# Moving the PSUM strip of a sequential recurrence's matmul from partitions 0 to 31 to partitions 96 to 127

## What is computed

```python
Wx = jnp.einsum('bti,hi->bth', x, W)
Wx = ((flat - mean) * jax.lax.rsqrt(var + BN_EPS) * gamma + beta).reshape(B, T, H)
Vt = V.T

def step(yt, wx_t):
    yt = jax.nn.sigmoid(wx_t + yt @ Vt)
    return (yt, yt)
...
_, ys = jax.lax.scan(step, y0, jnp.swapaxes(Wx, 0, 1))
```

## Time and profile before

| | |
|---|---|
| median of 3 runs | 986.31 us (983.46 to 988.56) |
| the profiled execution | 980.51 us |
| its span, first to last instruction | 978.7 us |
| mean granted TensorE clock over the span | 0.975 |
| PE / ACT / DVE / POOL busy | 900.6 / 447.5 / 414.0 / 239.3 us |
| the L2 recurrence, first matmul to last sigmoid | 411.9 to 901.3 us |

### The profile page before, as it was taken

The page is one execution under the profiler, slowest core; times in us unless marked ns, Lnnn a source line. Parts: engine busy times, 40 slices in busy tenths (PEclk is TensorE's granted clock), DMA queues, the critical chain, the costliest instruction groups (busy, mean ns, idle before and its releaser), DMA issues. The chain is left out here.

```text
span 978.7 us, 15448 instructions
## 1 busy us (share of the span) xinstructions
PE 900.6 (92%) x6248; PEld 514.2 (53%) x6248; DVE 414.0 (42%) x711; ACT 447.5 (46%) x1492; POOL 239.3 (24%) x144
## 2 busy tenths in 40 slices
PE   7958888889989987899999999999999999999976
PEld 4426766667754443344444444455555544554543
DVE  4599999999966645500000000002005400202753
ACT  4687777777735442233333333333333333334642
POOL 3239999999820000200000000000000000000410
PEclk9989999999999997899999999999999999999987
DMA  3020000000000000200000000000000000000000
GB/s 81 11 55 1 1 1 1 1 1 1 1 6 2 1 24 11 82 1 1 2 1 1 1 1 1 1 1 1 1 1 1 1 1 1 1 1 2 1 25 11
DMA packets 10320, 8.30 MB, mean 8 GB/s; under 512 B 7346, under 2 KB 8610, under 8 KB 10152
## 3 DMA queue, kind: packets, MB, share of 16 engines
q1 hardware_dynamic: 10248, 7.31, 3.1%
HBM read 5.47 MB, written 0.26 MB: 6 GB/s over the span
## 5 line engine op out<-in xcount | busy, mean ns | idle before, releaser
L906 PE MATMUL L2p_z<-stream 128*128 128x512 bf16 x943 | 366.8, 390 | 0.0
L948 ACT ACTIVATE L2yx<-L2p_z 32x2 f32<-32x2 f32 x1024 | 165.0, 161 | 323.3 <-PE L2p_z L925 323.2
L925 PEld LDWEIGHTS L2p_z<-L2yx,L2v 64*32 64x32 f32 x2048 | 137.7, 104 | 224.6 <-ACT L2yx L948 218.4
L925 PE MATMUL L2p_z<-L2yx,L2v 64*32 64x2 f32 x2048 | 225.5, 178 | 1.0 <-PEq L822 0.9
L787 POOL TENSOR_TENSOR hc<-hs,cb 128x1024 f32<-128x1024 f32 x64 | 149.4, 2361 | 4.5 <-DVE hs L728 4.5
L557 PEld LDWEIGHTS p_y<-ident,hc 128*128 128x128 f32 x1024 | 123.2, 192 | 16.4 <-POOL hc L787 8.6
L557 PE MATMUL p_y<-ident,hc 128*128 128x128 f32 x1024 | 125.4, 276 | 4.2 <-POOL hc L787 4.2
L1613 DVE COPY xn<-L2yx 32x512 f32<-32x512 f32 (+1 forms) x2 | 0.8, 384 | 302.7 <-ACT L2yx L948 302.7
L1613 POOL COPY xn<-L2yx 32x128 f32<-32x128 f32 x1 | 0.3, 282 | 484.2 <-SPq L1956 484.2
L728 DVE TENSOR_TENSOR_SCAN hs<-d_a,p_bb 128x1024 f32<-128x1024 f32 x48 | 109.8, 2286 | 6.3
L906 PEld LDWEIGHTS L2p_z<-stream 128*128 128x128 bf16 x943 | 90.2, 96 | 15.0
(11 more groups left out here) (515 smaller groups left out, 886.0 us busy)
## 6 DMA issues: line engine op xcount, KB each, us to landing
y_l<-in_pick SPq DMA_DIRECT2D x1, 768.0 KB
b_parts<-part SPq DMA_DIRECT2D x6, 128.0 KB, 2.4
c_parts<-part SPq DMA_DIRECT2D x6, 128.0 KB, 2.4
pos<-in_pos SPq DMA_DIRECT2D x1, 512.0 KB, 3.5
ao<-in_at_o SPq DMA_DIRECT2D x1, 512.0 KB, 4.0
L1w<-in_L_w SPq DMA_DIRECT2D x1, 297.0 KB
L3w<-in_L_w SPq DMA_DIRECT2D x1, 297.0 KB
x_tok<-in_x SPq DMA_DIRECT2D x2, 128.0 KB, 3.1
```

What stands on the lines that cost most here:

```text
L906: pe.matmul(p_z[:, 1, 0:each], stream[:, 0:128], stream[:, 0:each], start=True, stop=True)
L925: pe.matmul(p_step[:, t % 2], v[:, 0:C], yx[:, NB * t:NB * (t + 1)], start=True, stop=True).then_inc(s("preact"), 1)
L948: act.activation(yx[0:C, NB * (t + 1):NB * (t + 2)], p_step[:, t % 2], ACT.Sigmoid).then_inc(s("state"), 1)
```

## The change

One line: the view `p_step` starts at partition 96 (C is 32) in place of partition 0. The matmul's and the sigmoid's operands follow from it; the weights, the moving operand and the sigmoid's destination are the same.

```diff
@@ -894,7 +894,7 @@
                     HALF, BULK = T // 2, T - 128
                     FILL, STEP, WINDOW, LEAST = 512, 473, 3413, 3290
-                    p_step = p_z[0:C, 0].rearrange("p (n b) -> p n b", b=NB)
+                    p_step = p_z[3 * C:4 * C, 0].rearrange("p (n b) -> p n b", b=NB)
                     front = beside(s2, by_batch)
                     with nc.Block() as block:
                         @block.tensor
```

## The result

The changed kernel takes 986.46 us, median of 20 runs (983.39 to 992.28), against 982.41 us for the kernel before, now also of 20 runs (979.88 to 988.56). The ratio is 1.004, with a 95% interval of 1.0028 to 1.0052: slower by 4 us. The forecast's 986.3 lies next to the measured 986.46, but only because the three runs shown of before had a median of 986.31, which twenty runs put at 982.41. What was forecast was no change, and there is one, if a small one.

A forecast was written before the change was run, and what follows sets the result against it. The loop was taken as bound by two equal 0.47 us chains, PE's own and matmul to sigmoid. All four costs of strip 96 were 0, leaving the three-run median: 986.3 us, range 980 to 998.

The forecast's parts named there:

- The two chains of 0.47 us: In each loop step with a filler, two equally long chains, within 0.01 us, were said to bound the loop.
- PE's chain: From one step's weight load through the filler to the next step's weight load: 0.15 + 0.32, again 0.47 us.
- The result chain: Step's weight load and matmul, sigmoid, next weight load: 0.22 + 0.04 + 0.16 + 0.05 = 0.47 us.
- From matmul to result: Delay from the step's matmul end to the sigmoid's start: extra for strip 96 bounded 0 to 0.03 us, taken as 0.
- leaving the array: When the filler's weight load can start after the step's matmul: cost 0, with 0.01 us to either side.
- loading the weights: The step's weight load: bounds of 4 ns to either side for strip 96, taken as 0.
- The 0.06 and 0.07 of the earlier trace: Gaps in us from line 840's last strip 96 matmul to its consumer, against 0.04 for strip 0.
- ACT's read: The sigmoid reading PSUM strip 96 in place of strip 0: bounds 0 and 9 ns, taken as 0.
- The sign named for it: In the loop, a slow read was to show as sigmoids of 0.17, against 0.161 us before.
- a price for the shift: ACT reading one strip and writing another: three strips at 3 ns each would be 9 ns.
- The rival "ACT reads a far strip more slowly": Sigmoid in the loop: 9 ns by 938 steps are 8 us, total 994.7 us; chance 0.06.
- The sum: All costs over the loop's 1023 steps: 0 each, so the three-run median of 986.31 us became the forecast.

The follow-up runs named there:

- the first experiment: Kernel before plus small sigmoids from each PSUM strip and DVE copies behind the output stores; sigmoids 161, 163, 165, 166 ns; its total time means nothing.

## Why the prediction was wrong

- **The two chains of 0.47 us** were read rightly, and they are the finer half of the result. With strip 0 PE's chain is the longer by 472.2 - 470.3 = 1.9 ns. The result chain became 5.6 ns longer, 4.7 of them in the sigmoid; PE's chain covers 1.9, and 3.7 are left on the step.
- **From matmul to result, leaving the array, loading the weights**: 0 in each, as forecast. The filler's load behind the step's (150 ns) and the loads' durations didn't move, and the sigmoid starts 258 ns behind the step's first weight load with every strip. The 0.06 and 0.07 of the earlier trace rows were then not strip 96's doing; whether they belong to DVE or to the neighbouring matmuls stays open. The reading of the Trainium skill, "TensorE: Matmul & The Clock Gate", Part 2, step 4 (DRAIN), by which a later strip's result comes out later, shows in no run here.
- **ACT's read** is the step that failed: it was put at 0, and strip 96 costs ACT 5 ns a read (161 to 166 ns). The sign named for it came, sigmoids of 0.17 us on the timeline. The bounds, 0 and 9 ns, held the 5 ns, but I took 0 "by line 884, the row of the same engine with equal times". Line 884 compares strips 0 and 32 only, and shows nothing of the 2 ns that the small sigmoids differ by between these two. In the first recurrence the same line's two reads took 808 and 805 ns, so 2 ns are below what it can show. Line 872 compares strips 64 and 96, on the other engine, and had 8 ns; DVE's copies in the first experiment differ by 12 ns between strips 0 and 96. I chose by the engine where the strip was the question. The reason given, a price for the shift, was wrong as well: the strip that is written changes the time by 2 ns at most, and strip 96 read without a shift (D to D) still takes 165.
- **The rival "ACT reads a far strip more slowly"**, with a chance of 0.06, is what happened, at 5 ns in place of 9. Its sum, 9 ns by 938 steps, took the whole of the cost to lie open, where PE's chain covers 1.9 ns; with the measured 3.7 ns a step it is 938 x 3.7 = 3.5 us. The half per cent below which nothing was to show is what three runs can tell; twenty runs tell 0.4%.
- **The sum** started from 986.31, which was 4 us above what more runs gave. That the forecast's figure came out is chance.

## What to carry to other kernels

Where a loop runs a thousand times through one small instruction, a row that says "no difference" has to come from the same operands, not only from the same engine: a few nanoseconds are below what a neighbouring pair shows, and a few small instructions at the kernel's end, repeated, measure them to a nanosecond. Before an extra of a few nanoseconds is added up, find the second chain beside the first: the shorter one's slack is given back, and only the rest is paid. For a small result that ACT or DVE fetches from PSUM in a tight loop, partitions 0 to 31 were the cheapest of the four places measured here.

## What was not expected of the hardware

Reading PSUM costs ACT 161, 163, 165 and 166 ns for 32 by 2 from partitions 0, 32, 64 and 96, to within 2 ns whatever strip is written, and DVE 148 and 160 ns from the first and the last. For ACT it is a price for each instruction, the same 5 ns with 512 columns; for DVE the first experiment tried only 2 columns. From SBUF, ACT takes 200 to 203 ns for the same, without such an order.

A filler 3% shorter (496 columns for 512) let the granted clock fall from 1.00 to 0.50 in the loop in the profiled executions, and cost 108 us by the median (1090.42 against 982.52); the shortest of its six runs, 993.0 us, is still above every run of the kernel before. In the step the filler looked as if it did nothing but fill a wait; it makes PE's chain as long as the result's, and a shorter one lost far more to the clock than it gave back in the steps.
